# Embedding tower: one order for gathers, stores and forms, and the sums of layer 0 on ScalarE

## What is computed

```
e  = stack([tbl_m[ids[:, m]] for m in range(32)], axis=1)      # 512 x 32 x 16
x0 = e; xk = e; outs = []
for W in (W0, W1, W2):            # (32, 32, 64), (32, 64, 64), (32, 64, 64)
    xk = relu(einsum('bmd,bhd,mhk->bkd', x0, xk, W))
    outs.append(sum(xk, axis=2))  # over d, 16 long
h = concat([concat(outs, axis=1), dense_ctx], axis=1)          # 512 x 208
y = relu(relu(h @ W_top1 + b_top1) @ W_top2 + b_top2) @ W_top3
```

## Time and profile before

| | us |
|---|---|
| three runs | 349.17, 349.21, 345.57 |
| median | 349.17 |
| profiled execution, its own time | 350.59 |
| its span, first to last instruction | 346.7 |
| outside the span | 3.9 |
| PE busy | 305.4 (88%) |
| DVE busy | 268.4 (77%) |
| POOL busy | 250.0 (72%) |
| ACT busy | 106.2 (31%) |
| mean granted TensorE clock | 0.985 |

### The profile page before, as it was taken

One profiled execution on the slowest core, in us unless ns is written; L12 is line 12 of the kernel. 1 busy time (PEld: TensorE's weight loads), 2 busy tenths in 40 slices (PEclk: granted clock), 3 DMA queues, 4 the chain that ended last, 5 costly groups with the idle time before them and its releaser, 6 DMA issues.

```text
span 346.7 us, 4323 instructions
## 1 busy us (share of the span) xinstructions
PE 305.4 (88%) x1482; PEld 114.3 (33%) x1482; DVE 268.4 (77%) x123; ACT 106.2 (31%) x478; POOL 250.0 (72%) x163
## 2 busy tenths in 40 slices
PE   0098889379899898999999999999999999999996
PEld 0054433125233322232333233323233333333444
DVE  0026849387997997999999999999999997981401
ACT  1001211200322532504262427242714277122112
POOL 5777738873978888898879887988890896947000
PEclk9999999859999999999999999999999999999999
DMA  5375964785969479529654964496358232210000
GB/s 181 37 264 94 361 169 133 227 256 108 312 257 196 87 259 367 117 53 366 229 130 99 385 173 118 111 382 179 97 165 317 65 88 66 52 38 2 0 0 0
DMA packets 55165, 56.68 MB, mean 164 GB/s; under 512 B 37894, under 2 KB 43912, under 8 KB 51944
## 3 DMA queue, kind: packets, MB, share of 16 engines
q1 hardware_dynamic: 41272, 39.92, 35.2%
q10 hardware_dynamic: 9776, 15.44, 16.9%
q0 software_dynamic: 4096, 1.06, 3.1%
HBM read 41.33 MB, written 2.10 MB: 125 GB/s over the span
## 4 chain that ended last, share of the span: by engine, by line
PE 63%; DMA 15%; DVE 8%; POOL 6%; issue 3%; ACTq 2%; SPq 1%; ACT 1%; DVEq 0%; POOLq 0%
PE result L669 55%; DVE z_vector L614 6%; DMA r_forms<-x_rows 6%; POOL gathered_rows L341 6%; DMA gathered_rows<-table,row_index 3%; DMA x_rows<-gathered_rows 3%; DMA xj_forms<-x_sb 2%; DVE z_vector L621 2%; PE left L723 2%; PE result L709 1%; PE result L738 1%; PE y_psum L738 1%; PE result L744 1%; PE y_psum L744 1%; PE left L796 1%
## 5 line engine op out<-in xcount | busy, mean ns | idle before, releaser
L669 PE MATMUL result<-z_vector,w_sb 128*64 128x512 f32 (+2 forms) x1024 | 206.3, 552 | 19.3 <-DVE z_vector L621 11.3
L614 DVE TENSOR_TENSOR z_vector<-left,r_forms 128x4096 f32<-128x4096 f32 (+3 forms) x44 | 168.3, 3869 | 10.8 <-PE left L723 6.9
L341 POOL DMA_INDIRECT gathered_rows<-table,row_index x128 | 121.8, 951 | 42.5 <-issue 34.5
L357 POOL TENSOR_TENSOR z_pool<-r_forms,xj_forms 128x2048 f32<-128x2048 f32 (+2 forms) x30 | 127.6, 4274 | 24.7 <-DMA xj_forms<-x_sb 18.2
L669 PEld LDWEIGHTS result<-z_vector,w_sb 128*64 128x64 f32 x1024 | 71.7, 138 | 148.6 <-issue 109.2
L621 DVE TENSOR_TENSOR z_vector<-left,r_forms 128x2048 f32<-128x2048 f32 (+4 forms) x52 | 88.8, 1759 | 32.8 <-DMA r_forms<-x_rows 26.8
L669 PE MATMUL result<-z_pool,w_sb 128*64 128x512 f32 (+2 forms) x240 | 51.4, 567 | 0.0
L423 ACT ACTIVATE x_sb<-result 128x512 f32<-128x512 f32 (+2 forms) x27 | 14.8, 549 | 102.5 <-PE result L669 91.0
L431 ACT ACTIVATE x_sb<-x_sb 128x16 f32<-128x16 f32 x168 | 33.4, 200 | 6.4 <-issue 6.4
L587 DVE TENSOR_REDUCE d_sums<-x_sb 128x32 f32<-128x512 f32 (+2 forms) x21 | 12.9, 619 | 24.7 <-ACT x_sb L423 24.7
L431 ACT ACTIVATION_READ_ACCUMULATOR x_sb<-x_sb 128x1 f32 x168 | 31.4, 187 | 0.0
(11 more groups left out here) (45 smaller groups left out, 53.0 us busy)
## 6 DMA issues: line engine op xcount, KB each, us to landing
r_forms<-x_rows SPq DMA_DIRECT2D x24, 1024.0 KB, 10.2
r_forms<-x_rows SPq DMA_DIRECT2D x8, 768.0 KB, 7.9
xj_forms<-x_sb ACTq DMA_DIRECT2D x24, 256.0 KB, 8.8
h_form<-x_rows SPq DMA_DIRECT2D x12, 256.0 KB, 3.1
xj_form<-x_sb ACTq DMA_DIRECT2D x12, 256.0 KB, 3.8
gathered_rows<-table,row_index POOLq DMA_INDIRECT x128, 3.5
r_forms<-x_rows SPq DMA_DIRECT2D x4, 512.0 KB, 6.1
x_rows<-gathered_rows SPq DMA_DIRECT2D x24, 64.0 KB, 2.7
```

The costliest lines, as they stand in the source:

```text
L341: nc.gpsimd.indirect_dma_start(gathered_rows[:, half % GATHERED, g], None, table, bass.IndirectOffsetOnAxis(ap=row_index[:, at:at + 1], ax ...
L357: nc.gpsimd.tensor_tensor(z_pool[:, unit % NZP, :, :, 0:columns(p)], r_forms(q, p)[:, :, s0:s1], xj1_forms[form_buffer(n, p)][:, :, 0:colu ...
L614: nc.vector.tensor_tensor(z_vector[:, unit % NV, :, 0:s1 - s0, 0:columns(p)], left[:, bank, :, 0:columns(p)].unsqueeze(2).broadcast_to([12 ...
L669: done = nc.tensor.matmul(result_of(n, p)[K * t:K * t + K, 0:columns(p)], weights, z[:, t, 0:columns(p)], start=first, stop=last)
```

## The change

- **Sums.** Layer 0's sums of pairs 2 to 7 move from DVE to ACT: 32 ACTIVATEs of 16 columns each, with the accumulator. Their copies are written to the buffer of layer 2, `x_sb[2]`, so ACT waits for layer 2's sums before them and for them before layer 2's relu. `sum_x3` becomes `sum_d(n, p, copied)`.
- **Copies.** ACT's `copy_xj1(1, p)` for p = 2 to 7 is taken ahead of these sums and ahead of layer 2's relu; for the last pair it now stands behind the sums of layer 2.
- **SP.** All pairs get the order that pair 0 had: store t0, load h t0, store t1, load r0 t0, load h t1, load r0 t1, load r1 twice. The six loads of the top weights move from ACT's list (in the middle of p = 2) to SP's (behind pair 5).
- **POOL.** `pool_chunks(1, 1)` is 0 and no longer 2: DVE makes all of that stage's products. The gathers of pair 3 join those of pair 2 ahead of the first products, each four with a wait on PE's use of a `z_vector` unit; the wait on the second `select` now stands ahead of pair 3 and no longer ahead of the last four gathers of pair 2. Stages (2,0) and (1,2) are followed by four gathers, the others by eight.
- **PE.** Layer 0 of pairs 0 and 1 is done with the two halves side by side, as for the others, when both halves are there. `busy(8)` is put behind stage (1,1).

```diff
 def pool_chunks(n, p):
-    few = {(1, 0): 0, (1, 1): 2, (2, 5): 4, (2, 6): 6, (2, 7): 6, (2, 8): 4}
+    few = {(1, 0): 0, (1, 1): 0, (2, 5): 4, (2, 6): 6, (2, 7): 6, (2, 8): 4}
...
             for p in range(1, NP):          # SP, before; p == 2 has its own order
-                    for t in range(2):
-                        store_x0(p, t)
-                    for t in range(2):
-                        load_h(p, t)
-                    for t in range(2):
-                        load_r0(p, t)
+            for p in range(NP):
+                store_x0(p, 0)
+                load_h(p, 0)
+                store_x0(p, 1)
+                load_r0(p, 0)
+                load_h(p, 1)
+                load_r0(p, 1)
                 for t in range(2):
                     load_r1(p, t)
+                if p == 5:
+                    load_top()
...
-            pool.wait_ge(selected, 1)
-            for k in range(4):
-                if k == 3:
-                    pool.wait_ge(selected, 2)
-                gather(GATHERS_BEFORE[4] + 4 * k, GATHERS_BEFORE[4] + 4 * k + 4)
-                pool.wait_ge(z_vector_used, k + 2)
-            first = GATHERS_FIRST
+            for p, used in ((2, VECTOR_BEFORE[1, 0] + 1), (3, VECTOR_BEFORE[1, 1])):
+                pool.wait_ge(selected, p - 1)
+                for k in range(4):
+                    gather(GATHERS_BEFORE[2 * p] + 4 * k, GATHERS_BEFORE[2 * p] + 4 * k + 4)
+                    pool.wait_ge(z_vector_used, used + k)
+            first = GATHERS_BEFORE[8]
             for n, p in STAGES:
                 if pool_units(n, p):
                     products(n, p)
-                    gather(first, first + 8)
-                    first += 8
+                    gathers = 4 if (n, p) in ((2, 0), (1, 2)) else 8
+                    gather(first, first + gathers)
+                    first += gathers
...
-            def sum_x3(p):
-                act.wait_ge(x_ready[2], p + 1)
+            def sum_d(n, p, copied):
+                act.wait_ge(x_ready[n], p + 1)
                 for b in range(SAMPLES[p]):
-                    rows = x_sb[2][:, D * b:D * b + D]
-                    done = nc.scalar.activation(rows, rows, ACT.Copy,
-                                                accum_out=d_sums[:, 2, START[p] + b:START[p] + b + 1])
-                done.then_inc(x_summed[2], 1)
+                    rows = slice(D * b, D * b + D)
+                    done = nc.scalar.activation(copied[:, rows], x_sb[n][:, rows], ACT.Copy,
+                                                accum_out=d_sums[:, n, START[p] + b:START[p] + b + 1])
+                done.then_inc(x_summed[n], 1)
...
             for p in range(NP - 1):
-                copy_xj1(1, p)
+                if p < 2:
+                    copy_xj1(1, p)
...
-                if p == 2:
-                    load_top()
...
+                if p > 1:
+                    sum_d(2, p - 2, x_sb[2])
+                if p > 0:
                     copy_xj1(1, p + 1)
-                if p > 1:
-                    sum_x3(p - 2)
-                if p > 0:
+                    if p + 1 < NP - 1:
+                        if p > 1:
+                            act.wait_ge(x_summed[2], p - 1)
+                        sum_d(0, p + 1, x_sb[2])
+                        act.wait_ge(x_summed[0], p + 2)
                     relu(2, p - 1)
...
-                        sum_d(0, p)
+                        if p < 2 or p == NP - 1:
+                            sum_d(0, p)
...
-            layer0_by_tile(0)
+            vector_unit(0, 0, 0)
+            squares(0)
...
-                if p == 0:
-                    layer0_by_tile(1)
-                else:
-                    vector_unit(0, p + 1, 0)
-                    squares(p + 1)
+                if p == 1:
+                    busy(8)
+                vector_unit(0, p + 1, 0)
+                squares(p + 1)
```

45 lines of the change are left out of this document (7 added, 38 removed).

## The result

The changed kernel took 336.28 us (median of 4 runs, 335.40 to 336.92) beside 349.19 us for the kernel before (4 runs, 345.57 to 349.90): ratio 0.965, 95% interval 0.958 to 0.972. The profiled execution of it took 335.40 us, with a span of 333.5 in place of 346.7, so 12.9 us less by the medians and 13.2 by the spans. The forecast was 338.2 us, with a range of 335.0 to 344.0.

A forecast was written before the change was run, and what follows sets the result against it. DVE was taken to bound the middle at 33.83 us a pair, PE close behind; after the change, POOL's gathers and r0. 10.7 us at pair 4 plus the repeat gave 11.0: 349.17 - 11.0 = 338.2 us, range 335.0 to 344.0.

The forecast's parts named there:

- The sum of 11.0: Whole kernel: total gain taken as 11.0 us, near the middle of 10.2 to 11.7.
- Pair 1, 1.1: Pair 1: r0 issued right behind the store, DVE's 0.89 us wait goes, second half about 1.1 us earlier.
- Pair 2, 6.3: Select of pair 2 at 76.9 us instead of 83.22, 6.3 earlier, pair 1's gain included.
- The top weights: Near 100 us: six issues leave ACT's queue, saving 2.13 us on DVE's path and 1.65 on PE's.
- The sums at 0.20: Layer 0's sums on ACT: 0.20 us each, so 32 take 6.4 us, which fit in its time.
- a pair at 33.24: Middle of the kernel: DVE, freed of a 0.59 us sum, takes 33.24 us a pair, not 33.83.
- rival D: ACT's sums take 0.31 us each beside PSUM traffic, delaying POOL's turns by 13.0 in all: 351.2 us, chance 0.03.
- Pair 4: Gathers end 7.1 us earlier, at 109.7; gather to product takes 13.7; DVE starts (0,4)'s second half at 123.4, 10.7 earlier.
- The repeat, taken at +0.3: Pairs 5 to 7: further gain of 0.3 to 1.0 us, with POOL's turn of 33.50 as the bound.
- the upper of my two ends: In the repeat: up to 0.59 us gained a pair while r0 lands in time, against 0.33 if POOL bounds.
- the step on pair 2's gathers: POOL's last four gathers of pair 2 no longer wait for the second select and start 4.8 us earlier.
- my rivals: Besides the forecast: later forms (0.24), PE's floor deciding (0.06), slower ACT sums (0.03), form 1 of (2,p) landing late (0.05).

The follow-up runs named there:

- undo_top: Changed kernel with the six loads of the top weights back on ScalarE's queue; 355.71 us, ratio 1.0046 to the kernel before at 354.12.
- after_again: The changed kernel itself, run again unedited on another chip; 355.59 us, ratio 1.0063 to the kernel before at 353.73.
- the first comparison: The original measurement of the changed kernel beside the kernel before: 336.28 against 349.19 us, ratio 0.965; which chip is not noted.
- undo_sp: Changed kernel with SyncE's old order of stores, h and r0 loads, top weights staying on SP; 359.25 us, ratio 1.0154 to before at 354.12.
- spread_steady: Changed kernel with three of the eight gathers behind layer 2's product moved between layer 1's products, from pair 3 on; 351.05 us, ratio 1.0035 to before.
- few_gathers: Changed kernel without most gathers from pair 2 on (42 of 128 remain, results false); 342.54 us, ratio 0.9676 to before at 354.04.

## Why the prediction was right, and where it holds

**The order of things** was right, as far as one trace of each kernel shows it: no wait before (0,2) and no fall of the clock, r0 of pair 4 as the last thing to come, and then a repeat at PE's and VectorE's floor. The sum of 11.0 was 2.2 short of the span's 13.2 (1.9 of the medians' 12.9). By its steps:

- Pair 1, 1.1: relu (0,1) starts at 45.18, in before at 46.76, 1.6.
- Pair 2, 6.3: 7.0. The second half was there at 63.39, expected 64; the dummies took 3.40 (15 of the 16 records), expected 3.7; PE began (0,2) at 66.63, expected 68.0; the clock stayed.
- The top weights: VectorE did not wait for ScalarE near 100, as forecast, and ScalarE's issues of 5 us are gone from in front of the copies. What this is worth in time was measured only where increments were held: undo_top's 1.0046 is no different from the changed kernel's 1.0063 there. The Trainium skill ("DMA: Bandwidth & Descriptors", section "Issuing engines are not separate DMA queues") calls the sequencer's time usually small, and by the total it is nothing there; but the trace of undo_top has the wait back. VectorE waits 1.63 us for the copy (117.89), and then 0.94 for a held increment (122.19), where after_again has no first wait and a second of 2.48 (until 121.41). So a wait for a held increment behind it hid the 1.63, and the 1.65 to 2.13 of the forecast is neither shown nor refuted for the first comparison.
- The sums at 0.20 and a pair at 33.24: 200 ns, and 33.23. The Trainium skill's budget of about 0.3 us for an ACTIVATE ("ScalarE: Activation LUTs", "Rules for kernel authors"), which the page gives for a bias handed over as a pointer, is too high for these 360, and rival D with it.
- Pair 4: its gathers were to come 7.1 earlier and came 10.7, for form 1 of (1,2) was there at 78.75 (I had said 80 to 82), and (2,1) did not wait for its own. The way from the gather to the product was to take 13.7 and took 16.0: 1.4 to the store, 4.8 until it had landed, 0.6 for h, 9.3 for r0. The gathers' own sum had a slip in it: 95 and a product of 3.5 make 98.5, not 99.6, so its steps give 108.6 and 8.2 earlier. For the way I had taken 2.96 for the landing, from pair 2's row, and not the 5.65 that pair 4's own row showed. The two errors work against each other, the gathers coming 3.6 earlier than forecast and the way taking 2.3 longer, so that 10.7 comes near 12.0 in part by luck: the mis-sized terms are these two.
- The repeat, taken at +0.3, brought 1.2: the lead at PE grew from 12.0 to 13.2 over two pairs, 0.6 each, the upper of my two ends. GpSimd's turn is 33.49 and it had slack enough not to bind.

**What no step of it held** is the condition. It was worked out from one trace, in which every increment came at once. On a chip where they did not, with before at 354 us, the same kernel gained nothing. In the step on pair 2's gathers, "that wait now stands behind them, so they start 4.8 us earlier" was true, and it was also what made the gathers one run of twelve, behind which relu (0,1) came 6 us late. None of my rivals had it; that the first comparison met the condition which the forecast took for granted was luck. It is a case in which a wait that is taken off one engine lengthens another's by a way that the program does not show.

**What the parts are worth there**, against the changed kernel's 1.0063, by their ratios (0.3 to 0.5% of uncertainty each, and all but the dummies across two chips): sums undone -0.55%, GpSimd's order undone -0.8%, top weights undone -0.2% (within error), SyncE's order undone +0.9%, dummies undone +0.55%. So the kernel is slower there without SyncE's new order and without the dummies, and faster with the sums or GpSimd's order undone. For SyncE's order that need not be the price of late forms: in the repeat of undo_sp VectorE waits 1.76 and 1.74 us for held increments (194.92 and 229.99); undo_top has nothing at the first of these places and 0.22 at the second. For the conditions of the first comparison the parts were not measured one by one; that stays open, apart from GpSimd's order, where spread_steady shows how much hangs on three gathers. By the ratios no kernel here comes near the changed one where nothing is held, and of those that do all the work none beats before clearly where increments are held.

## What to carry to other kernels

Find the transfer that ends last and count back from it to the last instruction that feeds it; a list of gathers is worth what its last member for the next pair is worth, not its mean rate. Run both kernels on more than one chip before a gain of a few per cent is believed, and look first at whether waits end when their work ends. Long unbroken runs of one engine's DMA issues should be suspected where signals come late; but a pause is paid by whoever waits for that engine next.

## What the runs showed of the hardware

On three chips (before at 353.7 to 354.1 us) waiters for TensorE's semaphore increments started up to 9 us after the last matmul while GpSimd issued gathers back to back: the most is relu (1,0) of undo_sp, at 55.65, with PE's last matmul for it ending at 46.47. Many started within some 3.5 us of a run's end (the run of undo_sp ends at 54.7), others inside a run, like relu (1,0) of after_again. It went on in the repeat, shorter: the select of PE ends at 188.19 in after_again, GpSimd's run of eight at 189.12, and VectorE starts at 191.09.

```profile
187.06 1.13 PE L696 MATMUL left<-x_sb,select_sb 64*128 64x512 f32 x4
...
188.18 0.94 POOL L334 DMA_INDIRECT gathered_rows<-table,row_index  x1 [0.30 <-issue]
...
191.09 8.76 DVE L603 TENSOR_TENSOR z_vector<-left,r_forms 128x4096 f32<-128x4096 f32 x2 [1.12 <-remote]
```

In the first comparison and on the fourth chip (349.2 and 350.0) it did not happen, though the changed kernel's gathers ran there until 68.7 us with no gap above 0.42, and spread_steady's from 29.6 to 69.3. few_gathers shows that it goes away with the gathers; that gathers are not enough for it, these two comparisons show. What the rest is stays open. One trait goes with it: DMA rows of the page, with the time from issue to landing as the last column, first of the changed kernel, then of its copy after_again.

```profile
gathered_rows<-table,row_index POOLq DMA_INDIRECT x128, 3.2
```

```profile
gathered_rows<-table,row_index POOLq DMA_INDIRECT x128
```

The copy's row has no landing time, because many of the semaphore events from which it is worked out are missing in that trace: it holds 2663 of them, the trace of the changed kernel, which is the same program, 5279. This goes with the chip in every run: the two traces of the first comparison and the two of the fourth chip hold 5279 to 5344 each, the nine full kernels on the other three 2616 to 2911, few_gathers 3419. So the path that records events lost records there, and may also have held back the engines. The Trainium skill ("NOTIFIC — the notification-queue block", section 7.1, "Overflow: three behaviours, one of which stalls the engine") says that the block that writes such records can stall what produces them when a queue of it fills. No run here shows that queue, and no execution without a recording was timed, so this is argued and not shown; lost records alone do not show that an engine was held. If it is so, part of the 354 us belongs to the measurement.
